# Down and out projections with the high and low weight parts in one matmul

## The reference, cut to what matters

```python
# experts: 8 experts, 1024 tokens each, F = 682
tokens = xf[idx]
mid = silu(einsum('keh,ehf->kef', tokens, Wu) + bu)
out = einsum('kef,efh->keh', mid, W_down) + b_down          # down projection
y = zeros_like(xf).at[idx].add(G[..., None] * out)          # G: the gate of a token
# mixer, its end
yn = group_norm(scan output) * gn_w + gn_b
out = yn * silu(z)                                          # z = xn @ Wz.T
s = out @ Wout.T                                            # out projection
x = x + s * silu(y)
```

## Time and profile before

| | us |
|---|---|
| runs without a profile, median of 3 | 1224.97 |
| the profiled execution, its own time | 1222.01 |
| its span, first to last instruction | 1220.2 |
| PE busy in the span | 1204.3 |
| VectorE busy | 955.1 |
| GpSimd busy | 798.3 |
| ScalarE busy | 612.8 |

### The profile page before, as it was taken

One profiled execution on the slowest core, in us unless ns is written; L12 is line 12 of the kernel. 1 busy time (PEld: TensorE's weight loads), 2 busy tenths in 40 slices (PEclk: granted clock), 3 DMA queues, 4 the chain that ended last, 5 costly groups with the idle time before them and its releaser, 6 DMA issues.

```text
span 1220.2 us, 31236 instructions
## 1 busy us (share of the span) xinstructions
PE 1204.3 (99%) x12207; PEld 1010.1 (83%) x12207; DVE 955.1 (78%) x2028; ACT 612.8 (50%) x1279; POOL 798.3 (65%) x790
## 2 busy tenths in 40 slices
PE   8999999999999999999999999999999999999998
PEld 4666668888888888888888887898899989899998
DVE  7999977898886677678778767987777775777676
ACT  6999984443444444344444445544333332555444
POOL 4889945545565576776776658467766645576774
PEclk9999999999999999999999999999999999999999
DMA  9799765644544544554554546565544446799995
GB/s 299 251 345 348 288 236 180 142 161 149 163 158 141 172 158 146 171 160 149 167 159 153 160 146 218 175 157 96 114 86 106 83 85 130 259 320 323 333 331 169
DMA packets 123122, 231.38 MB, mean 190 GB/s; under 512 B 22496, under 2 KB 81120, under 8 KB 118368
## 3 DMA queue, kind: packets, MB, share of 16 engines
q1 hardware_dynamic: 109824, 212.09, 52.0%
q0 software_dynamic: 12288, 17.05, 8.1%
q10 hardware_dynamic: 864, 0.24, 0.1%
HBM read 147.81 MB, written 81.53 MB: 188 GB/s over the span
## 4 chain that ended last, share of the span: by engine, by line
PE 85%; DVE 6%; DMA 3%; SPq 2%; ACT 2%; issue 1%; POOL 1%; ACTq 0%; DVEq 0%; POOLq 0%
PE ps L1443 26%; PE ps L1805 11%; PE ps L2064 9%; PE ps L2298 8%; PE ps L2277 7%; PE ps L1524 4%; PE ps L1491 3%; PE ps L1550 3%; PE ps L1513 3%; PE ps L1535 2%; PE ps L1564 2%; PE ps L695 1%; DMA parts_dram<-xn_lo 1%; PE ps L1784 1%; PE ps L1472 1%
## 5 line engine op out<-in xcount | busy, mean ns | idle before, releaser
L1405 ACT ACTIVATE decay<-tap,ncum 128x128 f32<-128x128 f32 x344 | 105.5, 389 | 170.0 <-POOL tap L1312 170.0
L1990 POOL DMA_INDIRECT ffn_dram<-ob,idx x64 | 109.8, 1716 | 82.3 <-DVE ob L1909 68.3
L2026 ACT ACTIVATE mid<-ps,b_up 128x512 f32<-128x512 f32 x96 | 66.2, 689 | 152.0 <-PE ps L1805 148.7
L1319 POOL TENSOR_TENSOR x_lo<-x,x_hi 128x512 fp32r<-128x512 f32 x56 | 77.1, 1378 | 99.8 <-ACT x_hi L1389 99.8
L1179 DVE TENSOR_TENSOR x_dt<-ps,dt 128x512 f32<-128x512 f32 x64 | 44.2, 691 | 115.0 <-PE ps L1550 114.7
L1443 PE MATMUL ps<-x_hi,w_hi_b 128*128 128x512 f32 x240 | 99.5, 415 | 0.0
L1443 PE MATMUL ps<-x_hi,w_hi_c 128*128 128x512 f32 x240 | 99.3, 414 | 0.0
L2153 POOL TENSOR_SCALAR yc<-yc,gn_scale,gn_shift 128x512 f32<-128x512 f32 x56 | 78.3, 1412 | 30.3 <-DMA yc<-y_dram 30.3
L1341 POOL TENSOR_SCALAR yb<-x,dcol 128x512 f32<-128x512 f32 x64 | 45.4, 711 | 79.5 <-DVE ystat L1205 59.2
L1443 PE MATMUL ps<-x_lo,w_hi_b 128*128 128x512 f32 x240 | 94.4, 393 | 0.0
L1443 PE MATMUL ps<-x_lo,w_hi_c 128*128 128x512 f32 x240 | 94.2, 392 | 0.0
(11 more groups left out here) (321 smaller groups left out, 3999.8 us busy)
## 6 DMA issues: line engine op xcount, KB each, us to landing
tap<-cum_dram SPq DMA_DIRECT2D x43, 512.0 KB, 4.1
x_dram<-x SPq DMA_DIRECT2D x16, 1024.0 KB, 5.7
ecum_row<-ecum_dram SPq DMA_DIRECT2D x128, 128.0 KB, 3.6
yc<-y_dram SPq DMA_DIRECT2D x16, 1024.0 KB, 6.6
y_dram<-yb SPq DMA_DIRECT2D x30, 512.0 KB, 2.8
x<-x_dram SPq DMA_DIRECT2D x26, 512.0 KB, 4.3
cum_row<-cum_dram SPq DMA_DIRECT2D x21, 512.0 KB, 4.2
rows_dram<-xn SPq DMA_DIRECT2D x16, 512.0 KB, 3.3
```

What stands on the lines that cost most here:

```text
L1319: nc.gpsimd.tensor_tensor(low, raw, high, ALU.subtract).then_inc(x_lo_ready, 1)
L1405: n = nc.scalar.activation(decay[g % 2][:, h, :], cum_row[g % NR][:, row, :], ACT.Exp, bias=t.ncum[:, g, h:h + 1])
L1990: pool.indirect_dma_start(out=t.ffn_dram, out_offset=bass.IndirectOffsetOnAxis(ap=t.idx[:, e, h * HC + c:h * HC + c + 1], axis=0), in_=ob[ ...
```

## The change

In both projections the high and the low weights are laid side by side in one tensor (`dn` for down, `wo` for out), and the high part of the tokens is multiplied with both in one matmul of 512 columns: columns 0 to 255 of the bank get high x high, columns 256 to 511 get high x low. The low part of the tokens times the high weights stays a matmul of 256 columns into the first half. The moving operand of the wide matmul is read in two runs of 256 elements, which lie 6 x 256 elements (down) or 4 x 256 elements (out) apart.

The two halves of a bank are summed behind: ACT takes the second half first (`weigh_half`, times the gate, into `ob`; in the output a plain copy into `oc`), then DVE adds the first half (`scalar_tensor_tensor` in `weigh`; in the output one add, and then the product with silu(ffn) from SBUF, two instructions in place of one). The last block of the output keeps three matmuls of 256 columns per slice and DVE's old order.

Further: the wait for the earlier scatter (`added`) moves from DVE to ACT; ACT waits for `gate_copied`; in pass 15 the second `xn_hi` of ACT stands behind four copies; `split_up_hi` and `split_out` of ACT stand behind copies too; ACT's first `split_down` and SP's `load_y(0)` have one wait more each, because dn, dn_raw1 and wo lie at other places; the semaphores cum_stored are one.

```diff
-    dn_hi = [padded("dn_hi0", [P, FT, s.D], F32R)]
+    dn_raw_1 = padded("dn_raw1", [P, FT, s.D])
...
-    t.wo_hi = sb("wo_hi", [P, MT, s.D], F32R)
+    t.wo = sb("wo", [P, 2, MT, s.D], F32R)
+    t.wo_hi, t.wo_lo = (t.wo[:, i, :, :] for i in range(2))
...
-    dn_hi.append(sb("dn_hi1", [P, FT, s.D], F32R))
-    dn_lo = [sb(f"dn_lo{i}", [P, FT - 1, s.D], F32R) for i in range(2)]
+    dn = [sb(f"dn{i}", [P, 2 * FT - 1, s.D], F32R) for i in range(2)]
+    dn_hi, dn_lo = ([a[:, i * FT:(i + 1) * FT - i, :] for a in dn] for i in range(2))
...
         def weigh(u, c):
             q, i = u % 2, u * HC + c
-            if u >= 2 and c == 0:
-                dve.wait_ge(added[q], 16 * HC * (u // 2))
-            dve.wait_ge(dn_mm, i + 1)
-            v.tensor_scalar(ob[q][:, c, :], ps_d[i % 3][:, 0:s.D], t.gate_col[q][:, c, :], None,
-                            ALU.mult).then_inc(out_ready, 1)
+            dve.wait_ge(half_ready, i + 1)
+            v.scalar_tensor_tensor(ob[q][:, c, :], ps_d[i % 3][:, 0:s.D], t.gate_col[q][:, c, :], ob[q][:, c, :],
+                                   ALU.mult, ALU.add).then_inc(out_ready, 1)
...
+                act.wait_ge(t.y_stored[0], 16 * 2 * (NB // 2))
...
+        def weigh_half(u, c):
+
+            q, i = u % 2, u * HC + c
+            if c == 0:
+                act.wait_ge(x.gate_copied, u + 1)
+                if u >= 2:
+                    act.wait_ge(added[q], 16 * HC * (u // 2))
+            act.wait_ge(dn_mm, i + 1)
+            nc.scalar.activation(ob[q][:, c, :], ps_d[i % 3][:, s.D:2 * s.D], ACT.Copy,
+                                 scale=t.gate_col[q][:, c, :]).then_inc(half_ready, 1)
...
             if h == NH - 1 and e + 1 < E:
                 split_down(e + 1)
-            if (u + 2) % (GS * NH) == 0 and u < last - 1:
-                x.split_up_hi(act, (u + 2) // (GS * NH))
+            for c in range(HC):
+                weigh_half(u - 1, c)
+                if c == 1 and (u + 2) % (GS * NH) == 0 and u < last - 1:
+                    x.split_up_hi(act, (u + 2) // (GS * NH))
+            if u == last:
+                o.xn_hi(act, 1)
+                for c in range(HC):
+                    weigh_half(last, c)
...
+                both, half = ps_d[i % 3].rearrange("p (i d) -> p i d", i=2), ps_d[i % 3][:, 0:s.D]
                 for f in range(FT - 1):
-                    for k, (a, wgt) in enumerate(((mid_hi[q], dn_hi[w]), (mid_lo[q], dn_hi[w]),
-                                                  (mid_hi[q], dn_lo[w]))):
-                        pe.matmul(ps_d[i % 3][:, 0:s.D], a[f][:, cs], wgt[:, f, :], start=(f == 0 and k == 0),
-                                  stop=False)
-                mm = pe.matmul(ps_d[i % 3][:, 0:s.D], mid_hi[q][FT - 1][:, cs], dn_hi[w][:, FT - 1, :],
-                               start=False, stop=True)
+                    pe.matmul(both, mid_hi[q][f][:, cs], x.dn[w][:, f:f + FT + 1:FT, :], start=(f == 0),
+                              stop=(f == FT - 2), skip_group_check=True)
+                    pe.matmul(half, mid_lo[q][f][:, cs], dn_hi[w][:, f, :], start=False, stop=False,
+                              skip_group_check=True)
+                mm = pe.matmul(half, mid_hi[q][FT - 1][:, cs], dn_hi[w][:, FT - 1, :], start=False, stop=True,
+                               skip_group_check=True)
...
-                v.tensor_tensor(oc[p][:, c, :], ps_o[c][:, 0:s.D], fc[p][:, c, :], ALU.mult).then_inc(mul_done, 1)
+                total = ps_o[c][:, 0:s.D]
+                if b < NB - 1:
+                    total = oc[p][:, c, :]
+                    dve.wait_ge(copied, COPIED + CH * b + c + 1)
+                    v.tensor_tensor(total, ps_o[c][:, 0:s.D], total, ALU.add).then_inc(mul_step, 1)
+                    dve.wait_ge(mul_step, products(b, c) - 1)
+                v.tensor_tensor(oc[p][:, c, :], total, fc[p][:, c, :], ALU.mult).then_inc(mul_step, 1)
...
+            if b < NB - 1:
+                if b >= 2:
+                    act.wait_ge(out_stored[p], 16 * (b // 2))
+                for c in range(CH):
+                    act.wait_ge(mm_done, CH * b + c + 1)
+                    nc.scalar.activation(oc[p][:, c, :], ps_o[c][:, s.D:2 * s.D], ACT.Copy).then_inc(copied, 1)
...
                 if b:
-                    pe.wait_ge(mul_done, CH * (b - 1) + c + 1)
-                n = 0
+                    pe.wait_ge(mul_step, products(b - 1, c) - 1)
+                both, half = ps_o[c].rearrange("p (i d) -> p i d", i=2), ps_o[c][:, 0:s.D]
+                cols = slice(c * P, (c + 1) * P)
                 for k in range(MT):
...
+                    if b < NB - 1:
+                        pe.matmul(both, gh[p][:, k, cols], t.wo[:, :, k, :], start=(k == 0), stop=(k == MT - 1),
+                                  skip_group_check=True)
```

More of the change, by code:

```diff
@@ L2033, in _ @@
             else:
-                for b in range(2):
-                    o.xn_hi(act, b)
+                o.xn_hi(act, 0)
             if u == AFFINE:
@@ L2173, in phase_output, with products @@
     loaded = [sem(f"c_loaded{i}") for i in range(2)]
-    zs_ready, gate_ready, gated, hi_ready, lo_ready, mm_done, mul_done, sum_done = (
+    zs_ready, gate_ready, gated, hi_ready, lo_ready, mm_done, mul_step, sum_done = (
         sem(f"c_{n}") for n in ("zs", "gate", "gated", "hi", "lo", "mm", "mul", "sum"))
-    last_sum = sem("c_last_sum")
+    last_sum, copied = sem("c_last_sum"), x.half_ready
+    COPIED = HC * NU
     out_stored = [sem(f"c_out{i}") for i in range(2)]
+    def products(b, c):
+        return 2 * (CH * b + c + 1) if b < NB - 1 else 2 * CH * b + c + 1
     def parts_loaded(b):
@@ L2212, in _ @@
                 dve.wait_ge(mm_done, CH * b + c + 1)
-                v.tensor_tensor(oc[p][:, c, :], ps_o[c][:, 0:s.D], fc[p][:, c, :], ALU.mult).then_inc(mul_done, 1)
+                total = ps_o[c][:, 0:s.D]
[5 more added lines that the diff above has]
+                v.tensor_tensor(oc[p][:, c, :], total, fc[p][:, c, :], ALU.mult).then_inc(mul_step, 1)
                 if b == NB - 1:
-                    dve.wait_ge(mul_done, CH * b + c + 1)
+                    dve.wait_ge(mul_step, products(b, c))
                     v.tensor_tensor(oc[p][:, c, :], oc[p][:, c, :], xc[p][:, c, :], ALU.add).then_inc(last_sum, 1)
@@ L2256, in _ @@
             if b < NB - 1:
-                pool.wait_ge(mul_done, CH * (b + 1))
+                pool.wait_ge(mul_step, products(b, CH - 1))
                 nc.gpsimd.tensor_tensor(oc[p][:, :, :], oc[p][:, :, :], xc[p][:, :, :], ALU.add).then_inc(sum_done, 1)
@@ L2293, in _ @@
                 if b:
-                    pe.wait_ge(mul_done, CH * (b - 1) + c + 1)
-                n = 0
+                    pe.wait_ge(mul_step, products(b - 1, c) - 1)
+                both, half = ps_o[c].rearrange("p (i d) -> p i d", i=2), ps_o[c][:, 0:s.D]
+                cols = slice(c * P, (c + 1) * P)
                 for k in range(MT):
-                    for g, w in ((gh[p], w_hi), (gl[p], w_hi), (gh[p], w_lo)):
-                        mm = pe.matmul(ps_o[c][:, 0:s.D], g[:, k, c * P:(c + 1) * P], w[:, k, :],
-                                       start=(n == 0), stop=(n == 3 * MT - 1))
-                        n += 1
+                    if b < NB - 1:
+                        pe.matmul(both, gh[p][:, k, cols], t.wo[:, :, k, :], start=(k == 0), stop=(k == MT - 1),
+                                  skip_group_check=True)
+                    else:
+                        for w in (w_hi, w_lo):
+                            pe.matmul(half, gh[p][:, k, cols], w[:, k, :], start=(k == 0 and w is w_hi), stop=False,
+                                      skip_group_check=True)
+                    mm = pe.matmul(half, gl[p][:, k, cols], w_hi[:, k, :], start=False, stop=(k == MT - 1),
+                                   skip_group_check=True)
                 mm.then_inc(mm_done, 1)
@@ L2334, in _ @@
         sp.wait_ge(x.dn_mm, HC * (NU - 2))
+        sp.wait_ge(x.dn_lo_ready, E)
         load_y(0)
@@ L2425, in build @@
             t.parts_stored = sem("parts_stored")
-            t.x2_back, t.cum_stored = ([sem(f"{n}{i}") for i in range(2)] for n in ("x2_back", "cum_stored"))
-            t.x1_lo, t.tile_out, t.gates_stored = (sem(n) for n in ("x1_lo", "tile_out", "gates_stored"))
+            t.x2_back = [sem(f"x2_back{i}") for i in range(2)]
+            t.x1_lo, t.tile_out, t.gates_stored, t.cum_stored = (
+                sem(n) for n in ("x1_lo", "tile_out", "gates_stored", "cum_stored"))
             t.turned, t.load_turned = turned_pair, load_turned
```

15 lines of the change are left out of this document (7 added, 8 removed).

## The result

The changed kernel takes 1233.57 us (median, 1232.97 to 1234.19) against 1224.96 us for the kernel before in the same runs: a ratio of 1.0069, 95% interval 1.0059 to 1.0079. It is slower by 8.6 us. The prediction was 1220.4 us with a range up to 1225.4, so it was wrong in sign, and the time lies where its rival 3 put it (1233, chance 0.04). The profiled execution took 1234.07 us with a span of 1232.2.

The account below looks back on a forecast made before the run. PE's own matmul stream was taken as the bound; 2.65 us from down behind pass 3 plus 2.9 from the output, less 1.0 in pass 3, gave 4.6 us saved: 1220.4 us, range 1218.0 to 1225.4.

Parts of the forecast that it names:

- rival 3: Output: DVE becomes the bound, its SBUF instructions stretching beside POOL; at 11.8 us a block, 1233 us; chance 0.04.
- The bound and the gain on PE: Down and output: PE's stream sets the time; wide plus narrow replaces three narrow, saving 10 and 12 ns a slice.
- The odd and even experts' two paces: Down: narrow matmuls take 120 ns in odd, 118 in even experts, so slices save 12 and 8 ns.
- The second run: Both projections: the wide matmul reading its weights in two runs of 256 was taken to cost nothing.
- rival 1: Second run costs what the instruction saved: 1226.0 us, chance 0.08; more than that, at 25 ns, 1233, chance 0.06.
- Rival 2: An instruction carries less than 12 ns in the mixed stream; with 3 ns saved a slice, 1224.3 us; chance 0.12.
- Pass 3: Down: ACT's copies behind Sqrt and split hold PE's fourth group, 1.0 us lost, and the gain up to there.
- hidden by the next Silu's time: Down: DVE's last group read comes 0.4 us later, but the next Silu needs 1.37 us of wide matmuls first.
- ACT's copy: Down and output: ACT's added copy of 256 columns from PSUM, 0.38 us each, 1.5 us per pass or block, hidden.
- Rival 4: Output: transfers already pace it, busy 0.91 at 322 GB/s; the 2.9 us go, 1223.3 us; chance 0.06.
- "Cost nothing" for DVE in the output: Four more adds bring DVE's block from 8.4 to 10.1 to 10.5 us of about 11.05, covered by idle time.
- the 0.8 of the forecast: Output: POOL's sum begins 0.8 us later, harmless since it had idled 1.58 us before it.

Follow-up runs that it names:

- second profile: The kernel before, without an edit, profiled again: 1223.83 us, span 1222.0.
- out_only: Changed kernel with the down projection's matmuls taken back to three narrow ones, new down weight layout kept: 1232.03 us, ratio 1.0066 to the kernel before.
- down_cont: `down_only` with high and low weights of a slice side by side, one run of 512 columns: 1223.08 us against 1223.05, ratio 1.0003.
- down_sqrt_late: `down_only` with pass 3's square root on ACT behind its four copies: 1222.44 us, ratio 0.9994.
- down_only: Changed kernel with the output stage taken back to what it was, only down changed: 1223.62 us against 1223.53 before, ratio 0.9999.
- pieces: Changed kernel, POOL adding each quarter right behind DVE's product of it, pass 3's square root behind ACT's copies: 1221.56 us against 1225.50 before, ratio 0.9970.
- out_tiny_sum: Changed kernel with POOL's sum of oc and xc shrunk to 8 columns, most of x missing from the output: 1220.37 us, ratio 0.9980.
- out_no_add: Changed kernel without DVE's sum of the halves in the output, low part of the weights missing: 1220.23 us, ratio 0.9979.
- the two kernels with pieces: `pieces`, and the same with DVE's sum kept in the PSUM bank, so the product has one operand there: 1221.46 us, ratio 0.9969.
- best_late: Changed kernel, POOL's sum waiting for DVE's four products yc times zs, pass 3's square root behind ACT's copies: 1226.64 us, ratio 1.0030 to the kernel before.

## Why the prediction was wrong, point by point

**The bound and the gain on PE: right in kind, a little large.** The step from narrow to wide was read off rows 3 as 120 ns and came so, or at 117; that from wide to narrow is 231 to 233 ns in the median and not 228. In the output a block fell from 11.24 to 11.07 us, 0.17 / 16 = 10.6 ns a slice, for 12 forecast. In `down` ten passes, between the starts of two `up` blocks, show it, here in the kernel before (second profile) and after:

```profile
828.22 8.36 PE ps L1805 x36
...
995.92 8.36 PE ps L1805 x36
```

```profile
831.43 8.37 PE ps L1804 x36
...
997.88 8.37 PE ps L1804 x36
```

Ten passes took 167.70 us and take 166.45: 0.125 us a pass, 6.3 ns a slice, for 10 forecast. Over the passes behind the third that is 1.7 us and not 2.65. The odd and even experts' two paces, which I had added up apart, became one of about 349 ns. `out_only` shows where the rest went: with the new layout three narrow matmuls take 3 x 120 = 360 ns in every pass, so the wide one saves 11 ns against that, and the layout had first lost the faster pace that half of the passes had. The 36 wide matmuls of `up` kept theirs, 227 or 232 ns, as assumed.

**The second run: right.** `down_cont` settles rival 1: a moving operand of two runs of 256 columns in SBUF costs nothing over one run of 512. The Trainium skill says in "PSUM — Partial Sum Buffer", Specifications, that access patterns that are not contiguous slow matmuls significantly, and doesn't say on which operand. For this one the trace does not agree; other patterns were not tried. Rival 2 is half right: the wide matmul does run at over 230 ns in its new place, and the saving is less than 12 ns, but twice to three times its 3 ns. Its figure from the Trainium skill, "TensorE: Matmul & The Clock Gate", Back-to-back issue gap, 2.5 ns an instruction, is far under the 10.6 and 6.3 ns that were saved.

**Pass 3: half right.** I forecast a hold of PE before the fourth group by ACT's order, 1.0 us, and nothing gained up to there. PE waited 1.0 us for DVE's ob behind that order, at 829.30, and `down_sqrt_late` took the wait away. Not forecast was the gap of 0.6 us before the third group, where PE waits for DVE's read of the moments. Its root stands in the chain of the profile after at the head of the pass:

```profile
812.69 0.48 ACT ob L2020
813.20 0.48 DVE ob L1907
```

ACT's copy stands ahead of DVE's last weighing of the pass before. That weighing begins 0.7 us behind the first matmul of `up` (812.49), where it began 0.2 behind it before (809.39 and 809.19), and DVE, busy without a pause from there, reads the moments the same half microsecond later. I had called it hidden by the next Silu's time. The other passes show no loss from it, but in this one DVE has no pause in which to catch up. From `up` to `up` pass 3 takes 831.27 - 812.49 = 18.8 us and took 826.22 - 809.19 = 17.0; with these 1.75 us the gain of the other passes is spent: `down_only` stands at 0.9999.

**ACT's copy: right by luck.** The 0.38 us of a copy of 256 columns came out (378 ns), but the sum took the 1045 ns of L2248 for a read from PSUM; that row reads fc, which lies in SBUF.

**Rival 4: fell.** `pieces` moves 326 GB/s at a DMA share of 0.93, and PE is busy in all of the 95 us.

**The failed step: "Cost nothing" for DVE in the output.** I summed DVE's block from mean durations, 4 x 899 + 4 x 782 + 8 x 422 and waits, and got 10.1 to 10.5 us of 11.05. The new instructions cost 0.4 us a block more than priced, all in the first of the four products, which meets POOL's group norm; that alone would still have fitted. The error was to carry over 899 ns as if it belonged to the instruction. It is 0.69 us plus a collision, and the change moves the two parties of that collision: it puts POOL's sum later and eats the 1.72 us that DVE had idled. Both shifts stood in the same paragraph as harmless, each for itself. The numbers were there: in the earlier trace rows POOL's sum ran from 1121.95 to 1124.35 and DVE's pair from 1123.58, an overlap of 0.77 us, and the pair took 2.02 us against 1.28 alone, 0.74 more.

The first block after shows the first step. POOL's sum begins 1.9 us behind the first z piece of the chain (1057.19) and not 0.55 as before (1121.95 and 1121.40), so 1.3 us later and not the 0.8 of the forecast; DVE's pair still begins 2.2 us behind it, as before:

```profile
1059.37 3.25 DVE L2214 TENSOR_TENSOR yc<-yc,zs 128x512 f32<-128x512 f32 x2 [0.38 <-ACT zs L2262]
```

```profile
1059.07 2.40 POOL L2291 TENSOR_TENSOR oc<-oc,xc 128x1024 f32<-128x1024 f32 x1 [0.36 <-DVE oc L2240]
```

From the second block on DVE comes late and has no pause, and both begin together. Then the pair loses 3.50 - 1.28 = 2.2 us, 1.5 more a block than before. 10.3 + 0.4 + 1.5 = 12.2; the four means above give 4 x (1287 + 787 + 417 + 531) ns = 12.1. Such sums count the overlap of neighbouring records twice: DVE's busy time is 90.22 / 8 = 11.3 us a block, and with 0.6 of waits that is the 11.84 us of the blocks from 1104.52 to 1199.25, well past the 11.05 of PE.

Rival 3 named the place and the mechanism and got 0.04, since I saw idle stretches on DVE as a reserve, where they were what kept the two engines apart. That it also names the time is partly luck. By its own terms 8.4 us lost in place of 2.9 won make 1220.4 + 2.9 + 8.4 = 1231.7 and not 1233, it has all 15 blocks at 11.8 us where the lag reached PE only from the fifth on, and it knows nothing of the 3.6 us at the end.

**What was not forecast at all:** the pause at the end and the clock behind it, 3.6 us together, a consequence of the same lag: `out_tiny_sum`, `out_no_add` and the two kernels with pieces have neither.

## What to carry to other kernels

Before a mean duration goes into a sum, see in the timeline whether it holds a collision, and ask whether the change moves either party; an idle stretch between two engines that share a path is not free room. When an instruction of PE is traded for one on DVE, sum the receiving engine's block with the worst overlap and compare it with the new, shorter period of PE. If GpSimd must work over SBUF beside DVE, cut its work into pieces that run next to DVE instructions with an operand in PSUM: here that took the output stage from 192.8 to 181.7 us, and together with the later square root it turned +0.7% into -0.3% with nothing left out.

## What the runs showed of the hardware that was not expected

- A DVE `tensor_tensor` over two SBUF operands and a GpSimd instruction over SBUF do not share, they exclude each other, and the one that begins first goes on. In the profile after a single product of 512 columns, 0.69 us alone, took 2.87 us beside a sum of 2.77 us that was under way, and ended 0.54 us behind it. The sum takes 2.40 us when it begins before DVE's pair (1059.07) and 2.77 to 2.79 when DVE's first product is under way. DVE's instructions with one operand in PSUM kept 0.42 us beside the same engine. The Trainium skill has this as a rule in "SBUF — State Buffer", Who interferes with whom: the two engines' common pair of SBUF ports is an exclusive lock, and a DVE instruction with two SBUF inputs contends for it with a GpSimd one that reads SBUF. The trace agrees. Put to the overlap in the earlier trace rows, the rule would have pointed at the term that failed.

```profile
1071.75 2.87 DVE L2214 TENSOR_TENSOR yc<-yc,zs 128x512 f32<-128x512 f32 x1
```

```profile
1071.31 2.77 POOL L2291 TENSOR_TENSOR oc<-oc,xc 128x1024 f32<-128x1024 f32 x1 [3.02 <-DVE oc L2240]
```

- After PE had stood still for 2.2 us, its clock fell to the lower level for some 3 us, beginning 0.8 us after it had started again (from 1222.5); in `out_only` the same pause had the same consequence. The pauses of 1 us in pass 3, of 0.2 to 0.6 us in the output blocks and of 1.7 us in `best_late` left the clock at 1.00.
- PE pauses of 0.2 to 1.8 us in the middle of equal instructions, with no releaser, at 760 to 774 us, in other places and lengths from one execution of the same kernel to the next. Their cause stays open.
